# Residual add and row statistics at the end of each query group of attention: halved load, deferred statistics, last four tiles' statistics in the next phase

## What is computed

```python
# x: (16, 2048, 1024), float32
x = x + 0.5 * ffn(layernorm(x), w_gate, w_up, w_down)      # phase a1
x = x + attn(layernorm(x), Wq, bq, Wk, bk, Wv, bv)         # phases a2 (projections) and att
x = x + 0.5 * ffn(layernorm(x), w_gate, w_up, w_down)      # phase cs

def attn(...):   # 16 heads of 64
    w = softmax(einsum('bnhd,bmhd->bnmh', q, k) / 8, axis=2)
    return einsum('bnmh,bmhd->bnhd', w, v).reshape(B, T, D)
def ffn(...):    # hidden size 3072, weights int32 / 127
    return einsum('bsh,dh->bsd', silu(gate) * up, wd)
```

## Time and profile before

| | us |
|---|---|
| median of 2 runs | 4873.63 (4836.22 to 4911.04) |
| the profiled execution | 4442.41 |
| its span, slowest core (core 3) | 4440.9 |
| spans of the 8 cores | 4424.2 to 4440.9 |
| mean granted clock of TensorE, by core | 0.898 to 0.913 |
| PE busy | 3455.7 (78%) |
| ACT busy | 1377.9 (31%) |
| DVE busy | 1120.3 (25%) |
| DMA | 316.21 MB, 71 GB/s in the mean |

### The profile page before, as it was taken

One profiled execution on the slowest core, in us unless ns is written; L12 is line 12 of the kernel. 1 busy time (PEld: TensorE's weight loads), 2 busy tenths in 40 slices (PEclk: granted clock), 3 DMA queues, 4 the chain that ended last, 5 costly groups with the idle time before them and its releaser, 6 DMA issues. The chain is left out here.

```text
span 4440.9 us, 57363 instructions; the slowest of 8 cores (4424.2 to 4440.9 us)
## 1 busy us (share of the span) xinstructions
PE 3455.7 (78%) x22790; PEld 1653.4 (37%) x22790; DVE 1120.3 (25%) x1750; ACT 1377.9 (31%) x1630; POOL 144.6 (3%) x267
## 2 busy tenths in 40 slices
PE   3379799487776665898987979958777666589899
PEld 2234344132243333444443434423224333344444
DVE  3431211233312222212113121123331222221221
ACT  0021110000398886110102111010039888711010
POOL 3200000100000000000000000010000000000000
PEclk9999899798899898899998989979889888889999
DMA  7933221500000111333213322150000111033220
GB/s 241 283 92 114 86 76 43 119 19 10 20 6 34 39 39 41 93 116 94 76 44 94 118 87 76 43 119 19 10 19 1 39 39 39 32 99 118 95 76 38
DMA packets 264660, 316.21 MB, mean 71 GB/s; under 512 B 8904, under 2 KB 205512, under 8 KB 263376
## 3 DMA queue, kind: packets, MB, share of 16 engines
q1 hardware_dynamic: 238160, 230.74, 17.6%
q0 software_dynamic: 26240, 81.80, 5.9%
HBM read 255.89 MB, written 69.21 MB: 73 GB/s over the span
## 5 line engine op out<-in xcount | busy, mean ns | idle before, releaser
L960 ACT ACTIVATE att_eS<-PS,cb 128x1024 bf16<-128x1024 f32 x1024 | 1034.1, 1215 | 84.5 <-PE PS L946 84.5
L946 PE MATMUL PS<-Q,K 64*128 64x512 bf16 x2048 | 434.9, 418 | 292.7 <-ACT att_eS L960 282.3
L864 PE MATMUL PS<-V,att_eS 128*128 128x65 bf16 x8192 | 371.6, 203 | 76.1 <-DVE att_x2b L897 75.7
L864 PEld LDWEIGHTS PS<-V,att_eS 128*128 128x128 bf16 x8192 | 308.8, 103 | 208.8 <-issue 208.8
L478 PE MATMUL PS<-cs_xnfm,cs_wslg 128*128 128x512 bf16 x1536 | 369.7, 384 | 0.0
L478 PE MATMUL PS<-a1s_xnfm,a1s_wslg 128*128 128x512 bf16 x1536 | 369.6, 384 | 0.0
L484 PE MATMUL PS<-a1s_xnfm,a1s_wslu 128*128 128x512 bf16 x1536 | 364.2, 380 | 0.0
L484 PE MATMUL PS<-cs_xnfm,cs_wslu 128*128 128x512 bf16 x1536 | 364.0, 380 | 0.0
L495 ACT ACTIVATE cs_sg<-PS 128x512 bf16<-128x512 f32 x192 | 114.6, 597 | 756.0 <-PE PS L484 756.0
L522 PE MATMUL PS<-a1s_wdsb,a1s_hsb 128*128 128x512 bf16 x1536 | 333.8, 380 | 7.8 <-DVE a1s_hsb L501 7.8
L522 PE MATMUL PS<-cs_wdsb,cs_hsb 128*128 128x512 bf16 x1536 | 332.2, 379 | 7.5 <-DVE cs_hsb L501 7.5
(11 more groups left out here) (116 smaller groups left out, 2142.2 us busy)
## 6 DMA issues: line engine op xcount, KB each, us to landing
a1s_wslg<-wgT SPq DMA_DIRECT2D x48, 512.0 KB, 4.1
a1s_wslu<-wuT SPq DMA_DIRECT2D x48, 512.0 KB, 5.4
cs_wslg<-wgT SPq DMA_DIRECT2D x48, 512.0 KB, 4.1
cs_wslu<-wuT SPq DMA_DIRECT2D x48, 512.0 KB, 5.4
x1s<-a1s_xo POOLq DMA_DIRECT2D x32, 512.0 KB, 2.9
a2s_xst<-x1s SPq DMA_DIRECT2D x32, 512.0 KB, 3.3
att_x1q<-x1s SPq DMA_DIRECT2D x8, 2048.0 KB
x2s<-att_x2o POOLq DMA_DIRECT2D x32, 512.0 KB, 2.9
```

Of the source, the lines that this page charges most:

```text
L864: inst = e.matmul(PS1[:, (par * 2 + q2) * 512: (par * 2 + q2) * 512 + 65], expS[:, buf + kt * 1024 + par * 512 + qt * 128: buf + kt * 1024 ...
L946: inst = e.matmul(PS0[:, pp + par * 512: pp + (par + 1) * 512], K_sb[64 * par:64 * par + 64, hp * 2048 + r * 128: hp * 2048 + (r + 1) * 12 ...
L960: "scalar", lambda e, hp=hp, r=r, buf=buf, pp=pp: e.activation(expS[:, buf + r * 1024: buf + (r + 1) * 1024], PS0[:, pp:pp + 1024], AF.Exp ...
```

## The change

In attention, `x1q` shrinks from four tiles to two and `x2o` grows from two to four. A group's residual comes in two DMAs of 1 MB. The first is issued where the 2 MB one was; the second is issued by SP inside the drain, when the group's second add is done, and the third add waits for it. The drain keeps only the four adds and the four stores. The square and the two sums of a tile move to a new function, `stats_push`: for groups 0 to 2 they are emitted one tile at a time after the rounds of hp 1, 2, 3 and 4 of the next group. For group 3 they are not made in attention.

In phase cs three chains run at the start in place of four. The sums of tiles 12 to 15 and their chain are made in the phase, at the head of group 1, on DVE and ACT, with the code that phase a1 uses.

```diff
@@ ffn_phase @@
             if ext_stats:
-                for b_ in range(4):
+                for b_ in range(3):
                     t_statsdone[b_] = stats_chain(
...
-                    if not ext_stats:
+                    if not ext_stats or tt >= 12:
                         t_red[tt] = ph.op("vector", lambda e, tt=tt, xs_=xs_, xo_=xo_: e.reduce_sum(
                             sm_s[:, tt:tt + 1], xs_[:, xo_:xo_ + 1024],
                             axis=AX.X), deps=[t_load[tt]], inc="ev")
                         t_sq[tt] = ph.op("scalar", lambda e, tt=tt, xs_=xs_, xo_=xo_: e.activation(
                             sqscr[:], xs_[:, xo_:xo_ + 1024], AF.Square,
                             accum_out=sm_q[:, tt:tt + 1]),
-                            deps=[t_load[tt], t_sq[tt - 1] if tt >= 1 else None],
+                            deps=[t_load[tt],
+                                  t_sq[tt - 1]
+                                  if (tt >= 1 and (not ext_stats or tt >= 13))
+                                  else None],
                             inc="sc")
                         if tt % 4 == 3:
                             b_ = tt // 4
                             t_statsdone[b_] = stats_chain(
                                 ph, b_, t_red, t_sq,
-                                t_statsdone[b_ - 1] if b_ >= 1 else None)
+                                t_statsdone[b_ - 1] if b_ >= 1 else None,
+                                bufs=((sm_s, sm_q, sm2_m, sm2_r) if ext_stats
+                                      else None))
@@ attn_phase @@
-            nc.sbuf_tensor(nm + "_x1q", [128, 4 * 1024], F32) as x1q,
+            nc.sbuf_tensor(nm + "_x1q", [128, 2 * 1024], F32) as x1q,
...
-            nc.sbuf_tensor(nm + "_x2o", [128, 2 * 1024], F32) as x2o,
+            nc.sbuf_tensor(nm + "_x2o", [128, 4 * 1024], F32) as x2o,
@@ drain_qg @@
                     fi = qg * 4 + qt
-                    xsl = x2o[:, (qt % 2) * 1024:(qt % 2 + 1) * 1024]
+                    if qt == 2:
+                        t_x1[(qg, 1)] = ph.op("sync", lambda e, qg=qg: e.dma_start(
+                            x1q[:].rearrange("p (a t) -> p a t", a=2),
+                            x1s.ap().rearrange("(a p) t -> p a t", p=128)[
+                                :, qg * 4 + 2: qg * 4 + 4, :]),
+                            deps=[t_x2add[(qg, 1)]], inc=ph.ld("xq"), n=16)
+                    xsl = x2o[:, qt * 1024:(qt + 1) * 1024]
                     t_x2add[(qg, qt)] = ph.op("vector", lambda e, xsl=xsl, qt=qt: e.tensor_add(
                         xsl,
                         x2b[:, qt * 1024:(qt + 1) * 1024],
-                        x1q[:, qt * 1024:(qt + 1) * 1024]),
-                        deps=[t_yev[(qg, 7, qt // 2)], t_x1[qg],
-                              t_store.get(fi - 2), t_st2.get(fi - 2)], inc="ev")
+                        x1q[:, (qt % 2) * 1024:(qt % 2 + 1) * 1024]),
+                        deps=[t_yev[(qg, 7, qt // 2)], t_x1[(qg, qt // 2)],
+                              t_store.get(fi - 4), t_st2.get(fi - 4)], inc="ev")
...
+            def stats_push(qg, qt):
+                fi = qg * 4 + qt
+                xsl = x2o[:, qt * 1024:(qt + 1) * 1024]
+                nsl = nsq[:, (qt % 2) * 1024:(qt % 2 + 1) * 1024]
+                t_sm = ph.op("vector", lambda e, xsl=xsl, nsl=nsl: e.tensor_mul(
+                    nsl, xsl, xsl), ...)
+                ph.op("vector", ... e.reduce_sum(sm2_s[:, fi:fi + 1], xsl, axis=AX.X), ...)
+                t_st2[fi] = ph.op("vector", ... e.reduce_sum(
+                    sm2_q[:, fi:fi + 1], nsl, axis=AX.X), ...)
@@ the loop over qg and hp, after the 16 rounds of a head pair @@
                     pend[0] = (qg, hp)
+                    if qg >= 1 and qg - 1 < 3 and hp in (1, 2, 3, 4):
+                        stats_push(qg - 1, hp - 1)
                     if hp == 0 and qg > 0:
                         drain_qg(qg - 1)
-                        t_x1[qg] = ph.op("sync", ...  # 4 tiles, x1q
+                        t_x1[(qg, 0)] = ph.op("sync", ...  # 2 tiles, x1q
                             deps=[t_x2add[(qg - 1, 3)]], inc=ph.ld("xq"), n=16)
```

More of the change, by code:

```diff
@@ new lines, in drain_qg @@
+                    t_store[fi] = ph.op("gpsimd", lambda e, fi=fi, qt=qt, xsl=xsl: e.dma_start(
+                        x2s.ap()[fi * 128:(fi + 1) * 128, :], xsl),
+                        deps=[t_x2add[(qg, qt)]], inc=ph.st(f"o{qt}"), n=16)
+            def stats_push(qg, qt):
[3 more added lines that the diff above has]
+                t_sm = ph.op("vector", lambda e, xsl=xsl, nsl=nsl: e.tensor_mul(
+                    nsl, xsl, xsl),
+                    deps=[t_x2add[(qg, qt)], t_cb, t_st2.get(fi - 2)],
+                    inc="ev")
+                ph.op("vector", lambda e, xsl=xsl, fi=fi: e.reduce_sum(
+                    sm2_s[:, fi:fi + 1], xsl, axis=AX.X),
+                    deps=[t_x2add[(qg, qt)]], inc="ev")
+                t_st2[fi] = ph.op("vector", lambda e, nsl=nsl, fi=fi: e.reduce_sum(
+                    sm2_q[:, fi:fi + 1], nsl, axis=AX.X),
+                    deps=[t_sm], inc="ev")
@@ L937, in attn_phase @@
+            t_x1[(0, 0)] = ph.op("sync", lambda e: e.dma_start(
+                x1q[:].rearrange("p (a t) -> p a t", a=2),
+                x1s.ap().rearrange("(a p) t -> p a t", p=128)[:, 0:2, :]),
                 inc=ph.ld("xq"), n=16)
@@ L968, in attn_phase @@
                     pend[0] = (qg, hp)
+                    if qg >= 1 and qg - 1 < 3 and hp in (1, 2, 3, 4):
+                        stats_push(qg - 1, hp - 1)
                     if hp == 0 and qg > 0:
                         drain_qg(qg - 1)
-                        t_x1[qg] = ph.op("sync", lambda e, qg=qg: e.dma_start(
-                            x1q[:].rearrange("p (a t) -> p a t", a=4),
+                        t_x1[(qg, 0)] = ph.op("sync", lambda e, qg=qg: e.dma_start(
+                            x1q[:].rearrange("p (a t) -> p a t", a=2),
                             x1s.ap().rearrange("(a p) t -> p a t", p=128)[
-                                :, qg * 4: qg * 4 + 4, :]),
+                                :, qg * 4: qg * 4 + 2, :]),
                             deps=[t_x2add[(qg - 1, 3)]], inc=ph.ld("xq"), n=16)
```

## The result

| | before | changed |
|---|---|---|
| median of all timed runs, us | 4729.23 (11 runs, 4441.45 to 4911.04) | 4637.17 (12 runs, 4405.61 to 4916.32) |
| profiled execution, us | 4442.41 | 4407.06 |
| spans of the 8 cores, us | 4424.2 to 4440.9 | 4380.1 to 4405.3 |
| mean of the 8 spans, us | 4433.1 | 4393.7 |
| DVE busy, us | 1120.3 | 1099.7 |

The changed kernel takes 0.9926 of the time, 95% interval 0.9907 to 0.9946: 33 us less of 4442, interval 24 to 41. A second comparison, with other runs of both, gave 0.9917 (0.9898 to 0.9936), 37 us. It is faster, and by less than 2%. The medians of all runs say little: in some executions the cores of one die or of both are granted less clock (in the changed kernel's run of 4889.43 us cores 0 to 3 took 4386 to 4409 us at a mean of 0.90 to 0.91, and cores 4 to 7 took 4862 to 4888 us at 0.80), and the ratios leave those executions out.

What follows compares the result with a forecast made beforehand. PE bounds the feed-forward phases and ACT attention, with PE waiting for DVE's drains. 45.5 + 7.1 + 3.1 - 14.6 = 41.1 us, subtracted from the timed median 4873.6, gave 4832.5 us, range 4782 to 4896.

Steps and rivals of the forecast that it cites:

- The six waits: Attention's mid-phase drains: PE waits about 11.5 us each for DVE's normalisation; each drain 7.6 us shorter, 45.5 us in all.
- Three chains at the start of cs: Start of cs: the fourth chain goes, winning 1.53 us per sequence, 3.1 us in all.
- the piece at the head of group 1: Between the groups of cs: four row sums and a chain before the first normalisation, 7.31 us lost, twice, 14.6 us.
- The moved sums: Attention rounds: a tile's sums, 3.5 us, cost nothing while DVE's idle gap, 7.3 us on average, covers them.
- L: Drain: time from issue of the second 1 MB load to its landing, taken as 6.6 us, bounds 5.0 and 9.8.
- my own sum: Whole kernel: total gain written as 93.8 - 8L, 41.1 us at the L taken.
- The ends: End of attention, last drain: phase shorter by 4.35 us less 0.8 for a later-landing store; 3.55, twice 7.1 us.
- t+5.30+L: Last drain: when the last store goes out, t being the first add's start; it was 16.25 us after that add.
- rival 3: Drains: the stalls vanish, needing L = 2.6; gain 72 us, 4801; chance 0.06.
- rival 1: Drain: the halved load becomes the wait; slower from L = 11.7, 4893 us at 14.2; chance 0.06.
- Rival 2: Whole kernel: the time is paid back by less granted PE clock, time stays at 4874; chance 0.12.
- Rival 4: Attention rounds: moved sums hold PE; a batch of 8.3 us in a 7.3 gap would lose 24 us; chance 0.02.

Runs made afterwards that it cites:

- e6: Changed kernel with cs's sums of tiles 12 to 15 and their chain made between group 0's down matmuls; cs 557.7 and 558.6 us, 8.0 less each.
- e4: Changed kernel with all four tiles' sums after head pair 1, not one tile after each of 1 to 4; attention 621.4 and 621.6 us, 40.7 more together.
- e5: Changed kernel without the load in the drain: four-tile residual buffer, adds in place, next load issued early; ratio to the kernel before 0.9809.
- e7: e5 and e6 together on the changed kernel, with a1's sums also between group 0's down matmuls; ratio to the kernel before 0.971.
- e3: Changed kernel with the stores of a group's first two tiles held until the second half load landed; attention 592.9 and 594.9 us, 6.8 and 7.7 less.
- e1: Changed kernel without the cs part, last group's sums back at the end of attention; 11.6 us shorter by the stages, 9.7 by the mean span.
- e2: Kernel before with only the cs part: last four tiles' sums moved from attention to cs; 2.7 us won.

## Why the prediction was right and where it was wrong

**The mechanism: right, step by step.** The six waits were where the time was. The second load goes out 2.43 us after the first add (2.42 forecast). Three chains at the start of cs save 1.5 us, the piece at the head of group 1 costs 7.4 (7.31 taken from a1): cs as a whole is 5.8 us longer, and e6, which takes the piece away, makes it 8.0 us shorter. The moved sums are hidden by DVE's gap, and e4 shows that it is the gap that hides them. The gain is not paid back by the clock: e5 and e7 gain at least what was worked out for them.

**The term that was mis-sized: L.** I took 6.6 us. The runs show 7.5 in the mean over the eight cores (DVE's wait of 7.6 begins a little before the issue), and 6.6 to 9.6 from drain to drain on the slowest core. The shortest loads are the ones that I had summed up: 4.86 us without the stores (e3), where I had 5.0 as a bound (3.3 and 1.6 are 4.9), and 6.52 us beside them, where I had 6.6. What I left out is that most are longer, up to 7.55 and 9.60 us, so that the means are 5.5 and 7.5. The share of the stores is 2.0 us in the mean, where I had let half of their bytes count, 1.6. What makes the others longer is open. With L = 7.5 my own sum gives 93.8 - 60 = 33.8 us; the stages say 33.0, the two ratios 33 and 37. In the parts: attention was to win 52.6 us and won 44.6. The rule that spoke against the change, that SP's load shares the DMA engines with POOL's stores (the Trainium skill, DMA: Bandwidth & Descriptors, Queues, rings and completion order), agrees with e3, where the load is 2.0 us shorter without them; e3 shows the sharing, not that it goes packet by packet. The 28 us that I had worked out with both stores in full were off by 5, my 41 by 8. The estimate of 4.4 us for the load, from the Trainium skill (DMA: Bandwidth & Descriptors, Anatomy of one DMA), is 1.1 us short of the mean without the stores. The Trainium skill gives that fit there for transfers that GpSimd issues, and this load is SP's, so the estimate stood on less than I said.

**The ends.** The last store was to go out t+5.30+L and does (13.0 us for L = 7.7). That stores in close succession land later I had priced at 0.8 us. Over the cores and both sequences the phase ends 4.86 to 5.61 us after the last store, 5.05 in the mean, against 4.55 to 4.68 before: 0.5 us (0.3 on the core shown, 4.88 against 4.57). In e5, with four in a row, it is 1.3 us in the mean. The 16.25 us from first add to last store were the first sequence's; in the second it was 15.90, so that end had 0.35 us less to win.

**What went wrong is the place of the forecast.** I forecast 4832.5 us, 4782 to 4896, and the median of the changed kernel came out at 4637. The step that failed is the last of the sum: "The timed runs of before are 431 us longer", and "so I subtract the same microseconds", from 4873.6. That takes the 431 us for something that every timed run carries. I had taken the two runs shown, which lay 75 us apart, for the place where the kernel's time lies, and their half distance for its scatter. The runs show otherwise. Of the 11 runs of before three lie at 4441 to 4445 us and the others from 4513 to 4911; of the 12 of the changed kernel four lie at 4406 to 4416 and the others from 4580 to 4916. The 431 us came with the granted clock of single executions, and a median of all runs depends on how many of each kind it holds. Taken from the profiled execution my sum gave 4401.3 us, and the changed kernel's profiled execution took 4407.1; as a ratio the forecast was 0.991 and the result 0.993 and 0.992. The sum should have been bound to the profiled execution, and the range should have reached down to it.

**Small slips in the working.** Sixteen instructions of 1.13 us are 18.1 us, not the 18.86 of the drain; the rest are short waits between them, and the forecast rightly used the 18.86. In rival 3 the ends would give 15.1 us, not 14.9. Neither moves the forecast.

**The rivals.** The halved load did become the wait, as rival 1 said, but 4 us below the point at which it decides. Rival 2 falls with e5. Rival 3 needed a load of 2.6 us, shorter than any; e5 reaches its effect by another way and shows what the waits were worth. Rival 4's mechanism is real, as e4 shows with a batch of 13.6 us, but not at 3.5 us.

## What to carry to other kernels

Work on an engine that is busy a quarter of the time can still stand on the path: look for the instruction behind it that another engine waits for, and cut the work into batches that fit the gap before that instruction (3.4 us in a gap of 7 cost nothing, 13.6 cost 6.4). When a buffer has to be split for memory, look first for an update in place: it removed the load that the split had put into the drain, and 48 us with it, those of the shorter end of the phase included. And a piece of work moved out of one serial end into another is worth only the difference of the two; put it where its engine is idle anyway, as between the down matmuls.

## What the runs showed of the hardware

- A 1 MB load on SP's queue is used 5.5 us after its issue in the mean when the core's stores are held back until it has landed (e3, 64 loads, 4.86 to 7.55), and 7.5 us when two stores of 512 KB go out on POOL's queue within a microsecond of it (6.52 to 9.60). In each of the pairs of cores 0 and 1, 2 and 3, 4 and 5, 6 and 7 one core waits less than the other: 41.1 to 41.6 us over eight drains on cores 1, 2, 4 and 6, and 47.6 to 49.6 on cores 0, 3, 5 and 7 in e3; 57.8 to 59.4 us on cores 0, 2, 4 and 7, and 61.9 to 64.5 on cores 1, 3, 5 and 6 in the changed kernel. So it is not a property of a core. No run here tells why.
- A phase ends 0.3 us after DVE's last instruction where that is what it waits for (e1), and 4.6 to 4.7 us after the issue of a last store of 512 KB that comes 4.7 us behind the one before it (the kernel before). With one 1.1 to 1.9 us ahead of it, it is anything from 4.6 to 6.5 us (changed kernel 4.9 to 5.6, e2 4.6 to 6.1, e5 5.5 to 6.5).
